# Attention residual added in PSUM, token scales from the largest and smallest entry, integer token codes

## The reference

```python
Ix, Iy = sobel_x(x), sobel_y(x)
h = sum over the 3 channels of hypot(Ix, Iy)          # 16 x 256 x 256
h = concat([cls_tok, h], axis=1)                      # 257 tokens of 256
h = h + attention(layernorm(h), ...)                  # 16 heads of 16
h = h + ffn(layernorm(h), ...)
```

```python
scale = 127.0 / max(max(abs(x)), 1e-5)
xq = clip(round(x * scale), -128, 127) / scale        # x is layernorm(h)
```

## Time and profile before

| | us |
|---|---|
| median of 3 runs | 1623.98 |
| lowest, highest | 1623.11, 1624.61 |
| the profiled execution | 1622.37 |
| its span | 1620.3 |
| DVE busy | 1373.8 (85%) |
| PE busy | 839.6 (52%) |
| ACT busy | 699.8 (43%) |
| POOL busy | 110.1 (7%) |

### The profile page before, as it was taken

The page is one execution under the profiler, slowest core; times in us unless marked ns, Lnnn a source line. Parts: engine busy times, 40 slices in busy tenths (PEclk is TensorE's granted clock), DMA queues, the critical chain, the costliest instruction groups (busy, mean ns, idle before and its releaser), DMA issues.

```text
span 1620.3 us, 12694 instructions
## 1 busy us (share of the span) xinstructions
PE 839.6 (52%) x3318; PEld 655.5 (40%) x3318; DVE 1373.8 (85%) x2145; ACT 699.8 (43%) x1250; POOL 110.1 (7%) x154
## 2 busy tenths in 40 slices
PE   6663200466447743456537754256626764388543
PEld 3332100355336532344426543145525643376433
DVE  1999998899879999899879999899888999722676
ACT  1312332364375544164356553245446653132562
POOL 0000000001101000002101100002010100000000
PEclk9777655766569876667568976577568886577776
DMA  7000500013303510104302610104120300100001
GB/s 192 1 13 14 111 0 0 1 20 52 62 10 59 112 39 1 29 1 71 59 13 41 129 39 1 28 1 72 32 40 10 62 12 28 27 1 0 1 0 27
DMA packets 33421, 57.15 MB, mean 35 GB/s; under 512 B 6410, under 2 KB 23354, under 8 KB 31674
## 3 DMA queue, kind: packets, MB, share of 16 engines
q0 software_dynamic: 21024, 29.11, 11.1%
q1 hardware_dynamic: 12026, 26.31, 7.1%
q10 hardware_dynamic: 288, 0.79, 0.2%
HBM read 22.84 MB, written 4.25 MB: 17 GB/s over the span
## 4 chain that ended last, share of the span: by engine, by line
DVE 30%; issue 26%; ACT 15%; PE 12%; DMA 1%; DVEq 0%; ACTq 0%; SPq 0%
DVE arena L531 9%; DVE arena L528 6%; PE psum L1722 2%; ACT arena L1273 2%; DVE arena L872 2%; PE psum L1672 2%; PE psum L1694 1%; PE psum L1723 1%; PE psum L1576 1%; DVE red L544 1%; PE psum L1758 1%; ACT arena L1409 1%; ACT arena L1169 1%; DVE others L531 1%; ACT zT L1418 1%
## 5 line engine op out<-in xcount | busy, mean ns | idle before, releaser
L528 DVE TENSOR_TENSOR arena<-arena 128x768 f32<-128x768 f32 (+2 forms) x534 | 486.7, 967 | 45.8 <-ACT arena L1207 23.1
L531 DVE SCALAR_TENSOR_TENSOR arena<-arena 128x768 f32<-128x768 f32 (+2 forms) x224 | 201.4, 948 | 0.1
L1590 PE MATMUL psum<-zT,w1q 128*128 128x257 f32 x512 | 150.1, 431 | 41.8 <-ACT wout L1303 25.2
L1590 PEld LDWEIGHTS psum<-zT,w1q 128*128 128x128 f32 x512 | 111.3, 220 | 68.1 <-issue 27.5
L1576 PE MATMUL psum<-gpad,win 128*128 128x257 f32 x288 | 86.0, 442 | 54.9 <-ACT gpad L1285 54.9
L1238 ACT ACTIVATE arena<-arena 128x768 f32<-128x768 int16 x32 | 27.0, 843 | 175.6 <-DVE arena L531 175.2
L1694 PE MATMUL psum<-arena 128*128 128x257 f32 x128 | 50.6, 563 | 86.5 <-ACT arena L1392 65.3
L1576 PEld LDWEIGHTS psum<-gpad,win 128*128 128x128 f32 x288 | 62.6, 223 | 71.9 <-ACT gpad L1285 61.0
L531 DVE SCALAR_TENSOR_TENSOR arena<-img 128x768 f32<-128x768 f32 x88 | 79.5, 949 | 7.0 <-issue 6.4
L504 POOL DMA_DIRECT2D h<-others x60 | 51.7, 862 | 416.6 <-DVE others L531 347.7
L1169 ACT ACTIVATE arena<-arena 128x256 f32<-128x256 f32 x65 | 23.3, 409 | 118.4 <-DVE arena L531 68.2
(11 more groups left out here) (222 smaller groups left out, 1993.5 us busy)
## 6 DMA issues: line engine op xcount, KB each, us to landing
img<-x SPq DMA_DIRECT2D x36, 258.0 KB, 7.0
h<-others POOLq DMA_DIRECT2D x60, 128.0 KB, 2.7
arena<-nrows_mem POOLq DMA_DIRECT2D x18, 384.0 KB, 4.4
arena<-arena POOLq DMA_DIRECT2D x18, 384.0 KB, 4.1
arena<-img POOLq DMA_DIRECT2D x18, 384.0 KB, 4.9
out<-out SPq DMA_DIRECT2D x16, 256.0 KB
img<-x SPq DMA_DIRECT2D x48, 64.5 KB, 7.7
win<-w_in SPq DMA_DIRECT2D x4, 768.0 KB, 5.4
```

Source lines behind the costliest of these rows:

```text
L528: return v.tensor_tensor(o, a, b, op)
L531: return v.scalar_tensor_tensor(out=o, in0=a, scalar=s, in1=b, op0=op0, op1=op1)
L1590: ins = mm((A0, A1, B0, B1)[i % 4][:, 0:S], w1q[:, k, t * P:(t + 1) * P], zT[:, k, b, :], start=(k == 0), stop=(k == DT - 1))
```

## The change

It has four parts.

1. The attention residual. PE adds `out9` to PSUM itself: nine matmuls with the identity, before the output matmul, open the five banks, and the one-hot matmuls add to them. ACT reads the sums from PSUM, writes them into `out9` and sums the rows on the way. DVE's five additions are gone.
2. The largest absolute value. DVE takes the largest and the smallest entry of each row of `out9`, and from them and the mean the largest distance from the mean. The pass that subtracted the mean is gone.
3. Token codes. DVE writes `(out9 + nmean) * sc` as int16, which rounds it, into the room of `onehot` (`zi`); ACT multiplies the codes by `dq` into `zs`. DVE no longer waits for `zs`.
4. Slots of batch 3 in pair 1: on ACT `weights_transposed(3)` moves from slot 5 to slot 3, on DVE `own_heads(3)` from 6 to 7 and `context(3)` from 7 to 8.

```diff
--- before.py
+++ after.py
@@ -123,7 +123,7 @@
     U_STEPS = 56
     CARRIED_STEPS = 50
     NORM_STEPS = 50
-    G_STEPS = 44
+    G_STEPS = 46
     TILE_STEPS = 30
     IMG_IN = 16 * 2 * GB * CH
     FIRST_IN = 16 * GB * CH
@@ -170,7 +170,9 @@
         small = sb("small", [P, 16, ROW9])
         small2 = sb("small2", [P, 3, ROW9])
         token = sb("token", [P, 8, ROW9])
+        token2 = sb("token2", [P, 2, ROW9])
         onehot = sb("onehot", [P, ROW9, P])
+        zi = onehot.bitcast(I16)
         onehotT = sb("onehotT", [P, ROW9, P])[:, :, :]
         slot9 = sb("slot9", [P, ROW9])
         xT = sb("xT", [P, DT, GB, S])
@@ -354,8 +356,8 @@
         attnT_psum = sem("attnT_psum"); attnT_taken = sem("attnT_taken")
         ctx_psum = sem("ctx_psum"); ctxm_ready = sem("ctxm_ready"); pick_psum = sem("pick_psum")
         osel_psum = sem("osel_psum"); osel_ready = sem("osel_ready")
-        res_psum = sem("res_psum"); res_taken = sem("res_taken")
-        zs_ready = sem("zs_ready"); zT_psum = sem("zT_psum"); zT_taken = sem("zT_taken")
+        res_psum = sem("res_psum")
+        zi_ready = sem("zi_ready"); zs_ready = sem("zs_ready"); zT_psum = sem("zT_psum"); zT_taken = sem("zT_taken")
         g_psum = sem("g_psum")
         gd_ready = sem("gd_ready"); mid_ready = sem("mid_ready")
         y_conv = sem("y_conv"); f_ready = sem("f_ready")
@@ -997,22 +999,16 @@
                 stt(osel, A1[:, 0:D], 1.0 / S, osel, ALU.mult, ALU.add).then_inc(osel_ready, 1)
 
 
-                for k in range(5):
-                    dve.wait_ge(res_psum, g * 5 + k + 1)
-                    r0, r1 = 2 * k, min(2 * k + 2, ROW9)
-                    tt(out9[:, r0:r1, :], (A1, B0, B1, C0, C1)[k][:, 0:(r1 - r0) * D].rearrange("p (r n) -> p r n", n=D),
-                       out9[:, r0:r1, :], ALU.add).then_inc(res_taken, 1)
-
-
-                z = ln[0]
                 total, nmean, sq, rms, rstd, am, sc, dq = (token[:, k, :] for k in range(8))
+                top, low = token2[:, 0, :], token2[:, 1, :]
                 dve.wait_ge(sum2, g + 1)
                 v.tensor_scalar(nmean, total, -1.0 / D, None, ALU.mult).then_inc(mean2, 1)
+                step(v.tensor_reduce(top, out9[:, :, :], AX, ALU.max))
+                step(v.tensor_reduce(low, out9[:, :, :], AX, ALU.min))
                 dve.wait_ge(mean2, g + 1)
-                for row in range(ROW9):
-                    ins = v.tensor_scalar(z[:, row, :], out9[:, row, :], nmean[:, row:row + 1], None, ALU.add)
-                step(ins)
-                step(v.tensor_reduce(am, z, AX, ALU.max, apply_absolute_value=True))
+                step(tt(top, top, nmean, ALU.add))
+                step(tt(low, low, nmean, ALU.add))
+                step(stt(am, low, -1.0, top, ALU.mult, ALU.max))
                 dve.wait_ge(root2, g + 1)
                 step(v.reciprocal(rstd, rms))
                 step(tt(am, am, rstd, ALU.mult))
@@ -1021,12 +1017,9 @@
                 step(stt(sc, sc, 127.0, rstd, ALU.mult, ALU.mult))
                 step(v.tensor_scalar(dq, am, alpha[:, 0:1], None, ALU.mult))
                 for row in range(ROW9):
-                    ins = v.tensor_scalar(z[:, row, :], z[:, row, :], sc[:, row:row + 1], ROUND, ALU.mult, ALU.add)
-                step(ins)
-                for row in range(ROW9):
-                    ins = v.tensor_scalar(zs[:, row, :], z[:, row, :], ROUND, dq[:, row:row + 1], ALU.subtract, ALU.mult)
-                ins.then_inc(zs_ready, 1)
-                dve.wait_ge(zs_ready, g + 1)
+                    ins = v.tensor_scalar(zi[:, row, :], out9[:, row, :], nmean[:, row:row + 1], sc[:, row:row + 1],
+                                          ALU.add, ALU.mult)
+                ins.then_inc(zi_ready, 1)
 
             def norm_tokens(step, g, rows, before_y=None):
                 norm_rows(step, rows, g * 2 + 1, before_y)
@@ -1073,8 +1066,8 @@
                     if k == 4:
                         context(step, g, 2)
                         shares(step, g, 3)
-                    if k == 6: own_heads(step, g, 3)
-                    if k == 7: context(step, g, 3)
+                    if k == 7: own_heads(step, g, 3)
+                    if k == 8: context(step, g, 3)
                 return slot
 
 
@@ -1400,9 +1393,10 @@
 
                 total, nmean, sq, rms = (token[:, k, :] for k in range(4))
                 for k in range(5):
-                    act.wait_ge(res_taken, g * 5 + k + 1)
+                    act.wait_ge(res_psum, g * 5 + k + 1)
                     for row in range(2 * k, min(2 * k + 2, ROW9)):
-                        ins = s.activation(ln[1][:, row, :], out9[:, row, :], ACT.Copy, accum_out=total[:, row:row + 1])
+                        ins = s.activation(out9[:, row, :], (B0, C0, C1, T0, T1)[k][:, (row % 2) * D:(row % 2 + 1) * D],
+                                           ACT.Copy, accum_out=total[:, row:row + 1])
                 ins.then_inc(sum2, 1)
                 act.wait_ge(mean2, g + 1)
                 for row in range(ROW9):
@@ -1411,6 +1405,10 @@
                 ins.then_inc(squares2, 1)
                 act.wait_ge(squares2, g + 1)
                 s.activation(rms, sq, ACT.Sqrt, scale=1.0 / D, bias=col(K_EPS)).then_inc(root2, 1)
+                act.wait_ge(zi_ready, g + 1)
+                for row in range(ROW9):
+                    ins = s.activation(zs[:, row, :], zi[:, row, :], ACT.Copy, scale=token[:, 7, row:row + 1])
+                ins.then_inc(zs_ready, 1)
 
                 for i in range(4):
                     t, k = i // 2, i % 2
@@ -1450,7 +1448,7 @@
                         values(g, 3)
                     if k == 1: weights_transposed(g, 2)
                     if k == 2: exponentials(g, 3)
-                    if k == 5: weights_transposed(g, 3)
+                    if k == 3: weights_transposed(g, 3)
                 return slot
 
             for b in range(1, GB, 2):
@@ -1747,6 +1745,11 @@
                     weighted_values(b)
                 pick_queries(GB - 1)
 
+                pe.wait_ge(h_saved, g + 1)
+                for k in range(5):
+                    for r in range(2 * k, min(2 * k + 2, ROW9)):
+                        mm((B0, C0, C1, T0, T1)[k][:, (r % 2) * D:(r % 2 + 1) * D], ident, out9[:, r, :],
+                           start=(r % 2 == 0), stop=False)
                 pe.wait_ge(ctxT_ready, g * GB + GB)
                 for k in range(DT):
                     ins = mm(A0[:, 0:D], ctxT[:, k, :], wout[:, k, :], start=(k == 0), stop=(k == DT - 1))
@@ -1755,8 +1758,8 @@
                 pe.wait_ge(osel_ready, g + 1)
                 for k in range(5):
                     for r in range(2 * k, min(2 * k + 2, ROW9)):
-                        ins = mm((A1, B0, B1, C0, C1)[k][:, (r % 2) * D:(r % 2 + 1) * D], onehotT[:, r, :], osel,
-                                 start=True, stop=True)
+                        ins = mm((B0, C0, C1, T0, T1)[k][:, (r % 2) * D:(r % 2 + 1) * D], onehotT[:, r, :], osel,
+                                 start=False, stop=(r == min(2 * k + 1, ROW9 - 1)))
                     ins.then_inc(res_psum, 1)
 
                 pe.wait_ge(zs_ready, g + 1)
```

## The result

The changed kernel takes 1613.8 us (median of 5 executions, 1608.7 to 1614.9) where the kernel before takes 1624.0 (1622.5 to 1625.4). The ratio is 0.9933 with a 95% interval of 0.9918 to 0.9947: 10.2 us less, 2.3 less than forecast. The profiled execution of after took 1614.9 and its span is 1612.9.

What follows compares the result with a forecast made beforehand. It took DVE's waits and the chain through `nmean`, `zs` and the Abs as the bound, not DVE's sum. Loop groups -14.6 and last group +2.3 made -12.3 us from 1624.0: 1611.5 us forecast, own range 1606 to 1617.

Steps and rivals of the forecast that it cites:

- What bounds the kernel: From 443 to 478 a loop group is bound by the chain of `attend` up to the Abs, not DVE's sum.
- The two signs: Last group's pick to `nmean` growing by over 2 us, or DVE's wait at slot 5 or 6 exceeding 2 us.
- Slots of batch 3: Loop groups, before `own_heads(3)`: 5.05 us of DVE's wait go, 0.9 of the possible 5.9 lost to ScalarE's block.
- rival B: DVE's slot 5 or 6 waits 2 to 3 us longer for ScalarE: 1619 us, chance 0.12.
- Residual through PE: Behind the pick, identity matmuls cost 5.4 to 6.7 us; residual matmuls at the fast clock gain 1.6.
- rival A: PE's clock stays low in the identity block, output and residual matmuls: 1628 us, slower, chance 0.08.
- Sum on ScalarE: Last residual matmul to `nmean`: 0.6 us instead of 1.67 through a DVE add, 1.05 gained.
- From `nmean` to `zs`: Reductions hide before the root; behind it 6.1 us stand where 4.95 stood, 1.15 lost per group.
- Rival C: DVE's int16 pass runs at the slower rate: 1.25 us more in four groups, 1616.5 us, chance 0.17.
- The sum: Loop groups gain 14.6 us, the last group loses 2.3: -12.3 us, forecast 1611.5 us.

Runs made afterwards that it cites:

- slots alone: Only the slots of batch 3 moved, on the kernel before: 1612.3 us, ratio 0.9925.
- no slots: The changed kernel with the slots of batch 3 as before: 1631.9 us, ratio 1.0046.
- codes alone: The kernel before with only the largest and smallest entry, the integer codes and ScalarE's scaling pass: 1637.6 us, ratio 1.0086.
- float codes: The changed kernel with the codes written as f32, not rounded, into room of their own: 1617.6 us in one execution.
- fastest version: The changed kernel with codes and `zs` handed over by rows, transposes begun early, row copies ahead of batch 3's copies: 1591.9 us, ratio 0.9808.
- filler: The fastest version with one product per pair of image rows computed four times in PE's pause: 1596.2 us, ratio 0.9825.

## Why the prediction came out as it did

**What bounds the kernel**: right. The slots alone give the whole gain with DVE's work unchanged, and two kernels with less DVE work (no slots, codes alone) are slower than before. The two signs by which the forecast would have been wrong did not come: the last group's stretch from the pick to `nmean` grew by 0.15 us, and no wait at slot 5 passed 1.21.

**Slots of batch 3**: right in mechanism and place. The wait of `own_heads(3)` is gone three times. ScalarE's block at slot 3 cost DVE 0.79, 1.21 and 1.21 us at slot 5 where I had 0.9 (and "under 1 us" as a sign), so rival B, a new wait of 2 to 3 us, did not come. The working gave 0.4 us less to the third group alone, because the class token's transposes take 1.01 us there instead of 0.60; in the second they also take 1.01 (at 786.60 before), which I had not seen, and both groups show the longer wait. As an effect alone the slots were worth 11.3 us; the prediction never priced them alone.

**Residual through PE**: right. The block took 6.56, 6.63 and 6.68 us (5.4 to 6.7 foreseen) and 5.41 in the last group; the clock rose 5 us after its start, so rival A fell; the output matmul 1.03 (1.25), the wait of `osel` 1.06 to 1.17 (0.5 to 1.8), the residual matmuls 4.15 (4.1). In the last group the block cost the chain 0.15 us net where I took 1.1, because it ran at its lower bound, 5.41 us. That is luck of the profiled execution: with the float codes, which leave PE's work as it is, the block took 7.07 us there, and `nmean` came 1.8 us later after the selection than before. The loop groups gained 5.7 us on average up to `nmean` where I took 6.15, the middle of 5.5 to 6.8: there the block ran at its upper bound, 0.5 above my middle.

**Sum on ScalarE**: 0.84 us from the end of the last residual matmul to `nmean` where I took 0.6.

**From `nmean` to `zs`**: the order was right (the reductions end 0.63 us before the root comes, 0.45 foreseen; ScalarE's pass 3.70, 3.6 foreseen), the size was too small: 1.79 us lost in each group, not 1.15. That is the one mis-sized term that matters, 0.64 x 4 = 2.6 us. I took 2.45 us for the DVE pass, "since the two f32 passes differ from it only in the output's type". Their instructions also differ in a second column of scalars, and by the float codes and the passes of before that is the one difference left for the 0.54 us; the type cost nothing. Rival C had the right sign for a wrong reason, and half its size. The Trainium skill (VectorE: DVE Perf Modes, What auto-detection actually checks), by which the output's type in itself is no hindrance, agrees with the float codes: 405 and 409 ns.

**The sum**: in spans -7.4 us against -12.3. Of the 4.9 between them 2.6 are the passes, 0.9 the stretch to `nmean` in the loop groups (17.1 gained, 18.05 foreseen), 1.7 what is given back behind the transposes, and 0.7 the start of the first group; the last group's attention was 1.0 better than foreseen. The median is nearer to the forecast (-10.2) than the profiled execution, which happened to be the slowest of five. Being only 2.3 us off the median is therefore partly luck: the difference between executions, 2.8 us here, went my way.

**What the working left out**: it treated each group as fixed work that moves with the chain. The waits of 1.65 us in front of the next Abs, which come and go with PE's clock, were not in it. In the changed kernel none came; in the codes alone three did.

## What to carry to other kernels

Price an edit by the wait that ends last behind it, not by the busiest engine's sum: 18 us of work taken from an engine that is busy 85% of the span bought nothing that can be told, and three moved lines bought 11. Where work is handed from one engine to another in the middle of a chain, pass it on row by row in the same edit, since the hand-over, not the work, was the cost here: 10.3 us of the chain in the traces, and 5.3 more with the next consumer. The medians gained more, about 12 and 20 us, but the rest came with the clock of a stretch that the edits do not touch. And where TensorE pauses, look at its granted clock on both sides of the pause before and after the edit, because the same instructions cost 1.7 to 2 times as much at the lower level.

## What the hardware showed that I had not expected

- **A pause of PE has a price beyond itself.** After 3.59 us without a matmul the six instructions of L1581 took 2.60 us, after 1.00 and 1.91 us they took 1.57. Three redundant products of 0.9 us each, put into the pause, made the kernel 0.5% faster. The Trainium skill (TensorE: Matmul & The Clock Gate, HAM oscillation — how this bites in real kernels) describes such a loop, in which every pause lets the clock fall and the work behind it starts slow; these rows agree.
- **Work put in front can pay for itself.** The 18 identity instructions brought the output matmul from 2.07 to 1.03 us and the residual matmuls from 5.72 to 4.15, if they ended just before; with a pause of 6.93 us between, the second gain was gone (6.06).
- **Times come in steps.** Because of this an edit worth 1 us can cost or bring 1.65 us in each of three groups. In the last group the stretch from the selection to `osel` took 88.0 to 88.1 us in three traces of kernels with the identity block, and 91.2 to 94.3 in the other six. Executions of one kernel scattered by 6.2 us in the changed kernel, 6.7 in the fastest version and 9.3 in the one with filler, against 2.8 in the kernel before; but only by 1.0 to 2.0 in five other versions. In several kernels the fastest executions have the higher mean granted clock: 0.722 at 1608.7 us and 0.712 to 0.714 at the other four of the changed kernel, 0.724 to 0.728 and 0.719 to 0.720 in the fastest version, 0.729 to 0.730 and 0.720 to 0.727 with filler. The version without its slots does not show it (0.718 at 1628.2 us, 0.713 to 0.719 near 1632). That fits the clock as the cause and does not prove it: only one execution of each kernel has a trace.
- **A second column of scalars costs about 60 ns** in a tensor_scalar of 128x256 (405 to 409 ns against 346 to 348), whether it writes int16 or float32.
